# Attention with positions: denominators from columns of ones, division on turned results, and one product at the end of the unit before

## The reference

```python
x = _layernorm(src, ln1_g, ln1_b)
q = (x @ wq).reshape(Bs, Ss, H, HD)          # 16 heads of 8
k, v = ...                                    # the same with wk, wv
p = (pe @ wp).reshape(2 * Ss - 1, H, HD)      # positions
ac = einsum('bihd,bjhd->bhij', q, k)
bd_full = einsum('bihd,phd->bhip', q, p)
bd = bd_full[:, :, arange(Ss)[:, None], rel]  # by distance i - j
att = softmax((ac + bd) * scale, axis=-1)
attn_out = einsum('bhij,bjhd->bihd', att, v).reshape(Bs, Ss, Ds) @ wo
src = src + attn_out
x2 = _layernorm(src, ln2_g, ln2_b)            # then the selection of experts
```

## Time and profile before

| | |
|---|---|
| Median of three runs | 2733.53 us |
| Profiled execution | 2727.38 us, span 2725.6 us |
| Attention f4, scores from first to last | 837.4 to 1379.7 us |
| Attention f6, scores from first to last | 1927.3 to 2473.2 us |
| Busy share of the whole span | PE 89%, DVE 71%, ACT 58%, POOL 57% |
| Granted PE clock within both attentions | 1.00 |

### The profile page before, as it was taken

The page is one execution under the profiler, slowest core; times in us unless marked ns, Lnnn a source line. Parts: engine busy times, 40 slices in busy tenths (PEclk is TensorE's granted clock), DMA queues, the critical chain, the costliest instruction groups (busy, mean ns, idle before and its releaser), DMA issues. The chain is left out here.

```text
span 2725.6 us, 59982 instructions
## 1 busy us (share of the span) xinstructions
PE 2434.7 (89%) x19038; PEld 1833.9 (67%) x19038; DVE 1930.1 (71%) x5169; ACT 1583.6 (58%) x4641; POOL 1556.9 (57%) x2343
## 2 busy tenths in 40 slices
PE   7999799799977999999988988999799999998888
PEld 5788677578865777777776335665577777777733
DVE  5554388455446899999876456776589999987645
ACT  3332245333326999999930226777699999993022
POOL 4322666332325588888743655554567888884365
PEclk9999799899988999999999998999899999999999
DMA  3810366370005455555455126553445555545512
GB/s 121 316 77 1 75 141 141 121 300 1 1 28 134 122 137 140 140 138 135 128 184 152 45 63 141 115 112 83 105 128 134 139 137 137 140 130 176 161 52 64
DMA packets 302396, 326.64 MB, mean 120 GB/s; under 512 B 31718, under 2 KB 274150, under 8 KB 294902
## 3 DMA queue, kind: packets, MB, share of 16 engines
q1 hardware_dynamic: 252934, 280.83, 37.8%
q0 software_dynamic: 12288, 25.19, 3.3%
q10 hardware_dynamic: 36864, 16.79, 2.1%
HBM read 133.36 MB, written 185.01 MB: 117 GB/s over the span
## 5 line engine op out<-in xcount | busy, mean ns | idle before, releaser
L2073 DVE TENSOR_REDUCE a_nm<-a_sr 128x2 f32<-128x512 f32 x256 | 167.0, 685 | 69.9 <-PE a_sr L1805 68.9
L3202 POOL TENSOR_TENSOR f4o_kv<-a5b_room 128x256 f32<-128x256 f32 x192 | 140.2, 731 | 107.7 <-DVE a5b_room L3070 101.9
L3202 POOL TENSOR_TENSOR f6o_kv<-a5b_room 128x256 f32<-128x256 f32 x192 | 140.3, 731 | 98.2 <-DVE a5b_room L3070 92.1
L2973 ACT ACTIVATE f6a_pr<-f6a_sr,f6a_nm 128x256 f32<-128x256 f32 x384 | 181.6, 486 | 12.1 <-DVE f6a_nm L3058 11.2
L2973 ACT ACTIVATE f4a_pr<-f4a_sr,f4a_nm 128x256 f32<-128x256 f32 x384 | 181.6, 486 | 9.2 <-DVE f4a_nm L3058 7.6
L3070 DVE TENSOR_TENSOR a5b_room<-f4a_ur,f4a_turn 128x512 f32<-128x512 f32 x192 | 131.3, 684 | 44.5 <-PE f4a_ur L2815 44.2
L3070 DVE TENSOR_TENSOR a5b_room<-f6a_ur,f6l_turn 128x512 f32<-128x512 f32 x192 | 131.4, 684 | 35.2 <-PE f6a_ur L2815 34.7
L2838 PE MATMUL f4a_sr<-all_ks,all_qs 96*128 96x256 bf16 x512 | 143.7, 281 | 13.9 <-ACT f4a_pr L2973 10.4
L2838 PE MATMUL f6a_sr<-all_ks,all_qs 96*128 96x256 bf16 x512 | 144.1, 282 | 13.2 <-ACT f6a_pr L2973 10.0
L2855 PE MATMUL f6a_tr<-all_table,f6a_pr 128*128 128x128 f32 x1024 | 155.2, 274 | 0.0
L2855 PE MATMUL f4a_tr<-all_table,f4a_pr 128*128 128x128 f32 x1024 | 155.0, 274 | 0.0
(11 more groups left out here) (672 smaller groups left out, 8477.6 us busy)
## 6 DMA issues: line engine op xcount, KB each, us to landing
slots<-f_zero SPq DMA_DIRECT2D x100, 512.0 KB, 6.1
f4a_slide<-f4o_kv SPq DMA_DIRECT2D x64, 383.0 KB
f6a_slide<-f6o_kv SPq DMA_DIRECT2D x64, 383.0 KB
f4o_kv<-f4a_slide SPq DMA_DIRECT2D x64, 256.0 KB
f6o_kv<-f6a_slide SPq DMA_DIRECT2D x64, 256.0 KB
f4o_src<-slots SPq DMA_DIRECT2D x128, 64.0 KB, 2.3
slots<-f4m_y ACTq DMA_DIRECT2D x128, 64.0 KB, 2.4
f6o_src<-slots SPq DMA_DIRECT2D x128, 64.0 KB, 2.2
```

The source lines that it names most:

```text
L2073: nc.vector.tensor_reduce(nm[:, r // 2, t, at_:at_ + 2], sr[:, g % SB, :].rearrange("p (x s) -> p x s", x=2), AX.X, ALU.max, negate=True). ...
L2973: last = nc.scalar.activation(pr[:, n % 4, x, :], from_, ACT.Exp, bias=nm[:, n % SB, x:x + 1], scale=sign, accum_out=zs[:, b[1], t, h:h + 1])
L3202: nc.gpsimd.tensor_tensor(rr[:, o % RAW, :], tmp[:, o % 2, 0, :], tmp[:, o % 2, 1, :], ALU.add)\
```

## The change

`vm`, the values laid out for the product, gets columns of ones where it had zeros: in head group r = 0 and 1 at columns 16 and 17 of each quarter, in r = 2 and 3 at columns 0 and 1. The value product writes groups 0 and 1 into the left half of `y_ps` and groups 2 and 3 into the right half, so each half holds 16 result columns and 2 sums for every quarter. The exponentials no longer sum. In the finishing step ACT copies `y_ps` (unit 4), PE turns it in four pieces into the desk (unit 5), DVE takes reciprocals of the sums and multiplies into `yq`, PE turns `yq` back (unit 7), ACT copies it to `yn`, PE projects out (unit 9 in place of 6). The statistics move from unit 7 to 10, the residual update from 9 to 13, the normalisation from 9 to 12, the turned tokens from 12 to 14, the selection from 14 to 15 and the gate sum from 15 to unit 0 of the next step. `reach` is split: its first product is issued by `reached` at the end of the unit before.

The diff, without the renamed buffers and semaphores:

```diff
@@ -2266,7 +2266,12 @@
         nc = self.nc
-        nc.vector.memset(self.vm[:, :, :, :, :].rearrange("p a b c d -> p (a b c d)"), 0.0).then_inc(self.vm_zero, 1)
+        whole = self.vm[:, :, :, :, :]
+        nc.vector.memset(whole.rearrange("p a b c d -> p (a b c d)"), 0.0).then_inc(self.vm_zero, 1)
+        dve.wait_ge(self.vm_zero, 1)
+        for first in (16, 2 * C):
+            nc.vector.memset(bass.AP(whole.tensor, whole.offset + first, [list(whole.ap[0]), [QUAD * C, 2 * TT], [C + 1, 2],
+                                                                         [QUAD * HD, QUAD]]), 1.0).then_inc(self.vm_zero, 1)
         nc.vector.tensor_copy(self.pe_hi[:, :], self.yn[:, :]).then_inc(self.pe_split, 1)
@@ -2662,13 +2666,13 @@
-                    [("count", 5, SENT), ("counts", B + 1, 1), ("table", B + 2, 1), ("rz", 3, B), ("v", 1, B), ("o", 3, B),
-                     ("ends", B + 1, 1), ("xt", 0, B), ("qk", 0, B), ("x2t", 3, B),
+                    [("count", 5, SENT), ("counts", B + 1, 1), ("table", B + 2, 1), ("v", 1, B), ("yt", 3, B), ("yb", 3, B),
+                     ("ends", B + 1, 1), ("xt", 0, B), ("o", 3, B), ("qk", 0, B), ("x2t", 3, B),
                      ("sel", 3, B)], 1)
-        AT = {"xt": 8, "qk": 10, "x2t": 12, "sel": 14, "src": 11, "ln": 3}
+        AT = {"y": 4, "yt": 5, "yb": 7, "xt": 8, "o": 9, "qk": 10, "x2t": 14, "sel": 15, "src": 11, "ln": 3}
@@ -2816,15 +2820,14 @@
 
-            def reach(b, hs):
-
-                if nth_slid(b, hs) == 0 and not led:
+            def reach(b, hs, t):
+
+                if nth_slid(b, hs) == 0 and t == 0 and not led:
...
-                for t in range(TT):
-                    n, first = nth_unit(b, hs) + t, P * (TT - 1 - t)
...
+                n, first = nth_unit(b, hs) + t, P * (TT - 1 - t)
...
@@ -2861,36 +2864,43 @@
                 if r == 0 and later_than(b, 1):
-                    pe.wait_ge(yn_ready, b[0])
+                    pe.wait_ge(y_copied, b[0])
                 for st in range(TT):
...
                         q = slice(j * QUAD * HD, (j + 1) * QUAD * HD)
-                        mm = nc.tensor.matmul(y_ps[q, 0:T], vm[:, b[0] % 2, st, r, q], pts[:, r % 2, st, j, :],
+                        mm = nc.tensor.matmul(y_ps[q, r // 2 * T:(r // 2 + 1) * T], vm[:, b[0] % 2, st, r, q], pts[:, r % 2, st, j, :],
                                               start=(r == 0 and st == 0), stop=(r == QUAD - 1 and st == TT - 1),
...
                 b, e = new(it), finish(it)
-                if n == 3 and e:
-                    pe.wait_ge(rz8_ready, e[0] + 1)
-                    out = fill(it, "rz")
-                    for t in range(TT):
-                        mm = nc.tensor.transpose(out[:, t * P:(t + 1) * P],
-                                                 rz8[:, t, :, :].rearrange("p h d -> p (h d)"), k.ident)
-                    mm.then_inc(desk.filled, 1)
                 if n == VALUES - 3 and prep(it):
                     lead.project_values(pe, prep(it)[0], fill(it, "v")).then_inc(desk.filled, 1)
-                if n == VALUES - 1 and e:
+                if n == AT["yt"] and e:
+                    pe.wait_ge(y_copied, e[0] + 1)
+                    out = fill(it, "yt")
+                    for hf in range(2):
+                        for t in range(TT):
+                            o = (hf * TT + t) * P
+                            mm = nc.tensor.transpose(out[:, o:o + P], y_sb[:, hf, t * P:(t + 1) * P], k.ident)
+                    mm.then_inc(desk.filled, 1)
+                if n == AT["yb"] and e:
+                    pe.wait_ge(yq_ready, e[0] + 1)
+                    out = fill(it, "yb")
+                    for t in range(TT):
+                        mm = nc.tensor.transpose(out[:, t * P:(t + 1) * P], yq[:, t, :], k.ident)
+                    mm.then_inc(desk.filled, 1)
+                if n == AT["xt"] and b:
+                    pe.wait_ge(lead.xn_ready, b[0] * TT + TT)
+                    lead.turn_tokens(pe, b[0], fill(it, "xt")).then_inc(desk.filled, 1)
+                if n == AT["o"] and e:
+                    pe.wait_ge(desk.emptied, desk.done(it, "yb"))
                     out = fill(it, "o")
-                    pe.wait_ge(yn_ready, e[0] + 1)
                     for t in range(TT):
...
                     mm.then_inc(desk.filled, 1)
-                if n == AT["xt"] and b:
-                    pe.wait_ge(lead.xn_ready, b[0] * TT + TT)
-                    lead.turn_tokens(pe, b[0], fill(it, "xt")).then_inc(desk.filled, 1)
                 if n == AT["qk"] and b:
@@ -2911,13 +2921,18 @@
                 if b is not None and slides(hs):
-                    reach(b, hs)
+                    reach(b, hs, 1)
                 elif b is not None:
...
 
+            def reached(it, n):
+                b, hs = relating(it, n, AHEAD + 1)
+                if b is not None and slides(hs):
+                    reach(b, hs, 0)
+
...
@@ -2933,9 +2948,10 @@
                             values(finish(it), r)
+                    reached(it, n)
 
             pe.wait_ge(k.loaded, k.loaded_count)
-            run(step, related)
+            run(step, lambda it, n: (related(it, n), reached(it, n)))
 
@@ -2965,20 +2981,20 @@
                     act.wait_ge(tr[t].filled, b[0] * (NR // 2) + n // 2 - 1)
-                if n == 0 and later_than(b, 2):
-                    act.wait_ge(rz_ready, b[0] - 1)
                 for x in range(2):
-                    h = head_at(hs + x)
                     from_, sign = (minus[:, n % SB, :], -1.0) if slides(hs + x) else (sr.bank(b, n)[:, x * T:(x + 1) * T], 1.0)
-                    last = nc.scalar.activation(pr[:, n % 4, x, :], from_, ACT.Exp, bias=nm[:, n % SB, x:x + 1], scale=sign,
-                                                accum_out=zs[:, b[1], t, h:h + 1])
+                    last = nc.scalar.activation(pr[:, n % 4, x, :], from_, ACT.Exp, bias=nm[:, n % SB, x:x + 1], scale=sign)
                 last.then_inc(sr.emptied, 1)
...
                 b, p, e = new(it), prep(it), finish(it)
-                if n == 3 and e:
-                    bank = taken(it, "rz")
-                    copy(rzb[:, :], bank[:, 0:T]).then_inc(desk.emptied, 1)
+                if n == AT["y"] and e:
+                    act.wait_ge(av_done, (e[0] + 1) * QUAD)
+                    if e[0]:
+                        act.wait_ge(yq_ready, e[0])
+                    copy(y_sb[:, :, :].rearrange("p h t -> p (h t)"), y_ps[:, :]).then_inc(y_copied, 1)
+                if n == AT["yb"] and e:
+                    copy(yn[:, :], taken(it, "yb")[:, 0:T]).then_inc(desk.emptied, 1)
                 if n == VALUES - 3 and p:
@@ -2994,7 +3010,7 @@
                     lead.normal_tokens(act, b[0])
-                if n == 9 and e and kept(e):
+                if n == 12 and e and kept(e):
                     opening.normal(act, e[0])
@@ -3097,6 +3113,10 @@
                     far.cut(dve, ur_ps[:, 0, :])
+                i = it[0] - 4
+                if n == 0 and 0 <= i < B - 1:
+                    dve.wait_ge(desk.emptied, desk.done((it[0] - 1, (it[1] + 1) % 2), "sel"))
+                    opening.gate_sum(dve, i)
                 i = placed(it)
@@ -3130,23 +3150,31 @@
                     i, par = e
-                    if n == 1:
-                        dve.wait_ge(sr.emptied, sr.done(e, NR - 1))
-                        nc.vector.reciprocal(rz[:, :, :], zs[:, par, :, :]).then_inc(rz_ready, 1)
+                    if n == AT["yt"]:
+                        dve.wait_ge(desk.filled, desk.nth(it, "yt"))
+                        bank = desk.bank(it, "yt").rearrange("p (h g c) -> p h g c", h=2, c=QUAD * HD)
+                        for hf in range(2):
+                            last = nc.vector.reciprocal(rz[:, hf, :, :], bank[:, hf, :, 16 * (1 - hf):16 * (1 - hf) + 2])
+                        last.then_inc(rz_ready, 1)
                         dve.wait_ge(rz_ready, i + 1)
-                        nc.vector.tensor_copy(rz8[:, :, :, :], rz[:, :, :].unsqueeze(3).to_broadcast([P, TT, H, HD]))\
-                            .then_inc(rz8_ready, 1)
-                    if n == VALUES - 3:
-                        dve.wait_ge(av_done, (i + 1) * QUAD)
-                        dve.wait_ge(desk.emptied, desk.done(it, "rz"))
-                        nc.vector.tensor_tensor(yn[:, :], y_ps[:, 0:T], rzb[:, :], ALU.mult).then_inc(yn_ready, 1)
-                    if n == 6:
+                        if i:
+                            dve.wait_ge(desk.filled, desk.nth((it[0] - 1, (it[1] + 1) % 2), "yb"))
+                        for hf in range(2):
+                            last = nc.vector.tensor_tensor(
+                                yq[:, :, :].rearrange("p t (j c) -> p (t j) c", c=QUAD * HD)[:, :, 16 * hf:16 * hf + 16]
+                                .rearrange("p g (r d) -> p g r d", d=HD),
+                                bank[:, hf, :, 16 * hf:16 * hf + 16].rearrange("p g (r d) -> p g r d", d=HD),
```

(50 more changed lines are left out.)

## The result

The changed kernel takes 2760.14 us (median of 4 runs, 2757.67 to 2761.72) where the one before, run beside it, takes 2733.82. The ratio is 1.0100, 95% interval 1.0088 to 1.0112: slower by 1.0%, 26 us, and outside the range forecast.

A forecast was written before the change was run, and what follows sets the result against it. No single engine bounds it: PE paces one stretch of a sequence, DVE the other. Sequences 0.2 us shorter, 32 times, plus 2.6 at the ends gave -3.8 us: 2729.5 from the 2733.5 median, range 2703 to 2753.

The forecast's parts named there:

- B: Stretch from DVE's rotation in unit 8 to PE's distance product of unit 15; DVE sets the pace, 14.1 us forecast.
- The update took 0.57: Residual update in unit 13, right behind the maxima: 0.57 us assumed, so DVE's path is 2.3 and PE's 2.46 counts.
- The third rival: Residual update collides with GpSimd's work in unit 13, taking 1.30 or some 2.0 us: 2743 to 2758 us, chance 0.27.
- Stretch A: From PE's distance product of unit 15 to DVE's rotation in unit 8; PE sets the pace, staying at 20.15 us.
- the sums' 0.4: Accumulator reads leaving ACT's path between the value copy and unit 7's scores: 4 x 0.10 = 0.4 us saved a sequence.
- ScalarE as the bound: Rival: ACT is the true bound in the relative attention, 0.9 us won a sequence, 2707 us, chance 0.30.
- The desk: One bank: unit 10's query and key product waits for DVE's unit 9 sum; hidden, up to 0.8 a sequence if uncovered.
- The reach move: First band product issued at the preceding unit's end: costs and brings nothing; its rival said 2689 us, chance 0.03.
- The ends: After each stage's last sequence nothing covers the longer finishing chain: about 1.3 us more, twice, +2.6.
- The sum: Whole kernel: 32 x -0.2 + 2.6 = -3.8 us, forecast as 2729.5 from the median of 2733.5.

The follow-up runs named there:

- e4: Changed kernel with VectorE's residual sum s1 moved first in unit 9, ahead of the sums of masks and index search: 2730.01 us, ratio 1.0000 to before.
- e6: Changed kernel with GpSimd's root for the second normalisation moved from its unit 10 to 11: 2744 us, ratio 1.0036 to before.
- e2: Kernel before with only the residual update moved, from unit 9 to unit 13: 2719.11 us against 2732.33, ratio 0.9962.
- e9: Changed kernel with the sums of the exponentials put back into a tile that nothing reads: 2777.28 us, ratio 1.0160 to before.
- e1: Changed kernel with the residual update moved from unit 13 to unit 10, ahead of the statistics: 2726.71 us, ratio 0.9980 to before.
- e5: Changed kernel with the residual update in unit 10 ahead of the statistics and s1 first in unit 9: 2734.89 us, ratio 1.0015 to before.

## Why the prediction was wrong

**The step that failed** is in B, "The update took 0.57 ... I take 0.57, because that row has the place among its neighbours that unit 13 will have". It measured 2.09. From the rotation of unit 13 to PE's product of unit 15 B took 3.89 (1181.37 to 1185.26; forecast 2.46), and the update fills 2.00 of it. From unit 8 to unit 13 it took 12.27 (forecast 11.52): gate_one, which had no term, is 0.46 of that error, and the other 0.29 is about what e4 takes away between the same marks. The row was read by VectorE's neighbours. For an operation that GpSimd can hold, GpSimd's moment counts, and the change moves that: the root went from GpSimd's unit 7 to 10, behind later statistics, and I gave this move no price. That the root's place decides is shown for gate_one (0.42 in e6); for the update e6 went from 2.09 to 1.48 only, so what else moved GpSimd's moment is not shown. Where the update took 0.57 GpSimd had waited for VectorE's rotation before its sum (0.36 in e2, 1.14 in the rows below); where it took 2.09 and 1.48 it had not. e2 shows the row was right for the move of the update alone (0.57, and a period 0.67 shorter, as -1.23 + 0.57 would have it); in the changed kernel's own first sequence it is right too:

```profile
900.18 0.73 POOL L3227 TENSOR_TENSOR f4o_kv<-a5b_room 128x256 f32<-128x256 f32 x1 [1.14 <-DVE a5b_room L3086]
...
900.63 0.57 DVE L3189 SCALAR_TENSOR_TENSOR all_x<-f4o_s,all_x 128x256 f32<-128x256 f32 x1
...
900.87 0.92 POOL L3234 TENSOR_TENSOR f4a_rr_lo<-f4o_kv,f4a_rr_hi 128x256 fp32r<-128x256 f32 x1
```

**The third rival** was the case: its mechanism, its place and its upper size ("some 2.0, +1.2" on a sequence of 34.25; the sequence came 1.5 over that, gate_one's 0.46 with it). It stood at 0.27, and the range ended at 2753, inside the rival's own 2743 to 2758.

**Stretch A, 20.15:** 19.68. The terms that cancelled to nothing came to -0.5; single ones were not tried, but the sums' 0.4 was: e9 gives 0.34 in the period.

**ScalarE as the bound:** no. PE's weight loads wait 6 us less for exponentials, and nothing is won in B.

**The desk:** the forecast hid it and named 0.8 as the price without cover. PE waits 0.73 for it; worth some 0.3 to 0.4 on the changed kernel, nothing on e1 (e4, e5).

**The reach move:** the order of PE at the band products is the same before and after, so it should cost and bring nothing. That is argued from the order; no run undoes it alone.

**The ends:** +2.6 forecast; the profiles show +2.4 between the attentions and +4.6 behind the second, 2 of 26 in the medians. e2, which has the update's move but not the longer chain, has +0.2 and +4.8 by the same marks, so the second is not the chain's. What they are made of was not looked into.

**The sum:** 2733.5 - 3.8 is 2729.7, not 2729.5; nothing hangs on it.

**The whole:** without the time held the steady period is reckoned at 33.4 before and 33.6 after, a difference that the column can't tell from none. So division by columns of ones is worth about nothing in this kernel's steady sequences, as far as that reckoning goes; no run has it without collisions. What decided was which operations it left beside GpSimd. The Trainium skill, SBUF — State Buffer, section Who interferes with whom, says that a VectorE instruction with two SBUF inputs contends with a GpSimd instruction that reads SBUF, that the shared ports are an exclusive lock, and that issue order, not shape, decides who blocks. The traces agree on the contention, and that shape does not decide: one and the same instruction took 0.57 and 2.09 us. But in both cases GpSimd's sum had started first, and the update stood through one of GpSimd's instructions in the one and through three in the other; a rule by issue order alone does not tell the two apart.

## What to carry to other kernels

An operation of VectorE with two SBUF inputs has no duration of its own beside GpSimd: the update took 0.41 to 2.09 us in the steady sequences here, by tenths of a microsecond in when it starts. Put such operations where GpSimd must wait for VectorE anyway, or let GpSimd wait for them, and price each move on GpSimd's queue as a move of these operations too. And ask first whether the stretch is VectorE's: 0.5 us freed in A bought nothing.
